# Other tile numbers for the side stages of a two-layer vision tower on one core

## The reference

```
h = tok(x, W)                                      # (16, 1024, 64)
h = h + attn0(layernorm(h), qkv, proj, bias_table) # scores + a bias of period 7
h = h + ffn0(layernorm(h), routed + shared)        # 128 hidden, 2 layers, ReLU
h = h + attn1(layernorm(h), qkv, proj)
h = h + ffn1(layernorm(h), top-2 of 8 experts)     # GELU, 128 hidden each
```

## Time and profile before

| | us |
|---|---|
| median of 3 runs | 4194.81 |
| lowest and highest | 4194.46, 4199.51 |
| the profiled execution, its own time | 4199.6 |
| its span, first to last instruction | 4197.8 |
| PE busy | 3900.1 (93%) |
| DVE busy | 2903.8 (69%) |
| ACT busy | 2638.1 (63%) |
| POOL busy | 857.9 (20%) |

### The profile page before, as it was taken

How to read it: one execution, slowest core, us unless ns; L and a number is a source line. 1 busy time by engine, 2 the same in 40 slices (tenths; PEclk the granted TensorE clock), 3 DMA queues, 4 the chain that set the end, 5 groups by cost and what they waited for, 6 DMA issues and landing times.

```text
span 4197.8 us, 62363 instructions
## 1 busy us (share of the span) xinstructions
PE 3900.1 (93%) x21508; PEld 1308.8 (31%) x21508; DVE 2903.8 (69%) x4955; ACT 2638.1 (63%) x4768; POOL 857.9 (20%) x1263
## 2 busy tenths in 40 slices
PE   6988999999999999999999999999999999999897
PEld 3223333332333323333333333323323333332222
DVE  4866767676776777757677776777767677677672
ACT  0656666666666666666666666666666666666564
POOL 4122212121211312212122121312212122121211
PEclk7999999999999999999999999999999999999998
DMA  5113201222112122111222112122111222111100
GB/s 103 37 31 56 39 21 31 51 40 42 34 34 41 31 42 49 36 25 31 42 48 42 33 35 41 31 42 49 33 27 31 42 49 42 30 31 28 23 10 6
DMA packets 119067, 156.36 MB, mean 37 GB/s; under 512 B 24847, under 2 KB 66575, under 8 KB 118717
## 3 DMA queue, kind: packets, MB, share of 16 engines
q1 hardware_dynamic: 118753, 152.38, 18.8%
HBM read 120.01 MB, written 29.36 MB: 36 GB/s over the span
## 4 chain that ended last, share of the span: by engine, by line
PE 68%; ACT 7%; POOL 7%; issue 6%; DVE 6%; DMA 2%; SPq 1%; POOLq 0%; ACTq 0%; DVEq 0%
PE acc L911 18%; PE side_st L897 18%; PE nat L885 15%; PE side_st L854 3%; DVE tile_max L1294 3%; PE side_st L750 2%; ACT hidden L1073 2%; POOL ln_s L1392 2%; ACT prob L1101 2%; PE side_st L840 2%; PE side_st L727 2%; PE side_st L807 1%; DMA q_rows<-max_rows 1%; ACT hidden L1019 1%; SPq L607 1%
## 5 line engine op out<-in xcount | busy, mean ns | idle before, releaser
L1294 DVE TENSOR_REDUCE tile_max<-nat 128x1 f32<-128x512 f32 x4096 | 2602.3, 683 | 1142.4 <-PE nat L885 1108.5
L1101 ACT ACTIVATE prob<-side_st 128x512 f32<-128x512 f32 x4096 | 2226.0, 600 | 1412.1 <-PE side_st L897 1373.7
L897 PE MATMUL side_st<-q_rows,k_rows 99*128 99x512 bf16 x4096 | 1578.4, 388 | 62.6 <-ACT prob L1101 32.3
L885 PE MATMUL nat<-k_rows,q_rows 96*128 96x512 bf16 x4096 | 1548.1, 389 | 35.8 <-DVE tile_max L1294 25.7
L911 PE MATMUL acc<-prob,v_padded 128*32 128x512 f32 x8192 | 1108.3, 613 | 6.0 <-ACT prob L1101 5.1
L897 PEld LDWEIGHTS side_st<-q_rows,k_rows 99*128 99x128 bf16 x4096 | 400.3, 99 | 1309.5 <-ACT prob L1101 903.9
L885 PEld LDWEIGHTS nat<-k_rows,q_rows 96*128 96x128 bf16 x4096 | 404.6, 99 | 529.8 <-DVE tile_max L1294 288.3
L1455 POOL TENSOR_SCALAR max_parts<-neg_max 128x16 bf16<-128x16 f32 x128 | 26.2, 205 | 1896.2 <-DVE neg_max L1301 1895.0
L911 PEld LDWEIGHTS acc<-prob,v_padded 128*32 128x32 f32 x8192 | 162.6, 108 | 376.7 <-ACT prob L1101 197.2
L840 PE MATMUL side_st<-ln_rows,w 64*128 64x512 f32 x512 | 140.1, 624 | 28.3 <-ACT hidden L1073 22.8
L1380 POOL TENSOR_SCALAR ln_s<-ln_s 128x8 f32<-128x8 f32 x64 | 12.9, 202 | 709.4 <-DVE ln_s L1202 705.7
(11 more groups left out here) (124 smaller groups left out, 2074.9 us busy)
## 6 DMA issues: line engine op xcount, KB each, us to landing
q_rows<-q_scratch SPq DMA_DIRECT2D x576, 64.0 KB
k_rows<-k_scratch SPq DMA_DIRECT2D x192, 192.0 KB
x_rows<-in_x SPq DMA_DIRECT2D x62, 512.0 KB, 6.5
q_scratch<-hidden SPq DMA_DIRECT2D x32, 384.0 KB
k_scratch<-hidden SPq DMA_DIRECT2D x96, 128.0 KB
group_weights<-in_routed SPq DMA_DIRECT2D x64, 129.0 KB, 2.1
q_rows<-max_rows SPq DMA_DIRECT2D x512, 3.0 KB
out_h<-out_rows SPq DMA_DIRECT2D x16, 256.0 KB, 2.1
```

What stands on the lines that cost most here:

```text
L885: eng.matmul(NAT[use % len(NAT)][:, :], QA[u][0:K_NAT, h, c:c + P], KA[u][0:K_NAT, h, kh * 512:kh * 512 + 512], start=True, stop=True)\
L897: eng.matmul(RING[TILE_BANK[n0 + n]][:, :], KA[u][0:K_ALL, h, t * P:t * P + P], QA[u][0:K_ALL, h, half * 512:half * 512 + 512], start=True ...
L1101: eng.activation(prob[:, n % TILES, :], RING[TILE_BANK[n0 + n]][:, :], ACT.Exp).then_inc(exp_done, 1)
L1294: eng.tensor_reduce(mx[:, q % 2, j // 8, j % 8 // 2, j % 2:j % 2 + 1], NAT[use % len(NAT)][:, :], AX.X, ALU.max).then_inc(nat_free, 1)
```

## The change

The numbers in `side_schedule` change, and nothing else. In `middle_of` the numbers count from tile 133: TR of LN "a" 161 to 162, H1 165 to 166, L0 170 to 171, L1 176 to 177, TR "1" 203 to 204, QK of the second layer 207 to 210, QV 212 to 213. In the tail of layer 1, TR goes from 31 to 33, GATE 35 to 36, RANK 41 to 43, MT 45 to 47, FW 48 to 50, FY0 to FY8 51 + 3k to 53 + 3k, OUT 82 to 85. For item r + 2, LN2 goes from 111 to 114, TR 119 to 123, QK 123 to 127, QV 127 to 131, VC 131 to 134, SCR 135 to 139, RL 144 to 147. WCA goes from 120 to 121.

```diff
         for dn, name, *more in ((0, "CT"), (5, "OTR"), (8, "PROJ", 0), (13, "LN1", "a"),
-                                (20, "LN2", "a"), (21, "BO"), (28, "TR", "a"), (32, "H1"), (37, "L0"),
-                                (43, "L1"), (49, "WO"), (56, "LN1", "1"), (62, "LN2", "1"),
-                                (70, "TR", "1"), (74, "QK", 1), (79, "QV", 1)):
+                                (20, "LN2", "a"), (21, "BO"), (29, "TR", "a"), (33, "H1"), (38, "L0"),
+                                (44, "L1"), (49, "WO"), (56, "LN1", "1"), (62, "LN2", "1"),
+                                (71, "TR", "1"), (77, "QK", 1), (80, "QV", 1)):
...
-        put(31, "TR", r - 1, "m")
-        put(35, "GATE", r - 1)
-        put(41, "RANK", r - 1)
-        put(45, "MT", r - 1)
-        put(48, "FW", r - 1)
+        put(33, "TR", r - 1, "m")
+        put(36, "GATE", r - 1)
+        put(43, "RANK", r - 1)
+        put(47, "MT", r - 1)
+        put(50, "FW", r - 1)
         for k in range(E + 1):
-            put(51 + 3 * k, f"FY{k}", r - 1)
-        put(82, "OUT", r - 1)
+            put(53 + 3 * k, f"FY{k}", r - 1)
+        put(85, "OUT", r - 1)
...
-        put(111, "LN2", r + 2, "0")
-        put(119, "TR", r + 2, "0")
-        put(123, "QK", r + 2, 0)
-        put(127, "QV", r + 2, 0)
-        put(131, "VC", r + 2, 0)
-        put(135, "SCR", r + 2, 0)
-        put(144, "RL", r + 2, 0, every=1)
+        put(114, "LN2", r + 2, "0")
+        put(123, "TR", r + 2, "0")
+        put(127, "QK", r + 2, 0)
+        put(131, "QV", r + 2, 0)
+        put(134, "VC", r + 2, 0)
+        put(139, "SCR", r + 2, 0)
+        put(147, "RL", r + 2, 0, every=1)
...
-        put(120, "WCA", r + 1)
+        put(121, "WCA", r + 1)
```

## The result

The changed kernel takes 4064.74 us (median of 4 runs, 4061.33 to 4069.15) beside 4195.88 us for the kernel before (median of 4 runs, 4194.46 to 4199.51): ratio 0.9687, interval 0.9670 to 0.9704, 131 us less. The direction and the mechanism came as forecast. The profiled execution took 4061.33 us, its span is 4059.6 us, and the mean granted clock 0.982.

The account below looks back on a forecast made before the run. PE, busy 93% of the span, was taken to set the pace. Large steps -5.3, small gains -2.2 and CT +0.6 made -6.9 us a pair, -97 in all: 4098 us, range 4070 to 4148.

Parts of the forecast that it names:

- The large steps: Second layer's QK and QV, tiles 207 to 215: stall, half clock and ACT wait go, QV waits; -5.3 us a pair.
- The half clock: Beside TN's stall at tile 215: the drop to 1.2 GHz goes with the stall, 2.5 us a pair.
- The forecast new waits: PE waits 1.1 us at QV (213) for ACT and 0.6 us at CT (133) for DVE.
- small terms: Waits at TN 119, TR 33 and 162, MT, OUT and tile 96 go: 2.9 us a pair, counted as 2.2.
- first layer's start: Tiles 111 to 147: TN's 0.58 us wait at 119 goes, CT at 133 gets a new wait of 0.6.
- the discount: Small gains counted at three quarters, 2.2 of 2.9 us, because a PE that waits less meets ACT and DVE less drained.
- the lower end: All small gains full, no wait at CT and 0.5 at QV: -8.8 us a pair, 4072; range from 4070.
- H1's new wait: At tile 169, for ACT's two copies: same size as the 0.73 us wait at 181 that goes, so they cancel.
- B: Rival: crowding at tiles 127 to 141 makes CT and `nat` wait and lowers the clock, +3.8 us a pair, 4151; chance 0.08.
- C: Rival: OUT's store holds up the maxima's transfers that tile 96's scores wait for; slower, 4225 us; chance 0.04.
- D: Rival: the split still stands behind POOL work at 209, only the small gains are left, about 4175 us; chance 0.04.
- A: Rival: the wait moves to QV (1.5 us) and TN (0.5), the half clock stays at tiles 210 to 216; 4146; chance 0.12.

Follow-up runs that it names:

- experiment 11: The changed kernel with six extra POOL products ahead of the split of the maxima at tile 209, once a pair: 4118.59 us, ratio 0.9826.
- experiment 1: The kernel before with only TR, QK and QV of the second layer moved, to 204, 210 and 213: 4114.79 us, ratio 0.9809.
- experiment 2: The changed kernel with TR, QK and QV of the second layer back at 203, 207 and 212: 4136.65 us, ratio 0.9855.
- experiment 3: The kernel before with only the tail of layer 1 moved (TR 33 to OUT 85): 4148.23 us, ratio 0.9883.
- experiment 5: The kernel before with only TR 162, H1 166, L0 171 and L1 177 moved: 4185.00 us, ratio 0.9970.
- Experiment 8: The changed kernel with H1 back at 165 and L0 at 170, L1 staying at 177: 4052.89 us, ratio 0.9656.
- experiment 10: The changed kernel with five extra POOL products ahead of the split of the maxima at tile 209, once a pair: 4100.81 us, ratio 0.9777.
- experiment 6: The changed kernel with QV of the second layer two tiles earlier, at 211: 4093.77 us, ratio 0.9753.

## Why the prediction was right, and where it was not

**The large steps held in their mechanism.** POOL's order at 209 was the cause of the stall at 215: with the order turned, TN waits for nothing, and six extra POOL operations ahead of the split bring a stall of 2.85 back (experiment 11). The half clock went with the stall in experiment 1 (3.4 us in one pair were left) and stood with it in experiment 2; the stall of 2.85 brought it back in a part of the pairs only. The forecast new waits came where they were named: 1.03 at QV (forecast 1.1, from ACT's 1.44 of copies in the earlier trace rows), 0.77 at CT (forecast 0.6, bounds 0 to 1.2). TR, MT and OUT show no wait at 33, 47, 85 and 162. What the sum lacked is size, in its small terms above all:

| place in a pair | forecast, us | measured, us |
|---|---|---|
| late stages, tiles 192 to 223 | -5.3 | -6.1 |
| tail and tile 96, tiles 16 to 95 | 2.07 x 3/4 = -1.6 | -3.1 |
| first layer's start, tiles 112 to 143 | -0.58 x 3/4 + 0.6 = +0.2 | 0.0 |
| middle, tiles 160 to 191 | -0.29 x 3/4 = -0.2 | -0.6 |
| a pair | -6.9 | -9.8 |

Measured is the median over pairs 2 to 12 of the spacing of scores, segment by segment. Over the whole profiled execution pairs 1 to 13 give 126 us (forecast 90), pair 0 gives 7.0 (5), the last pair and phase 3.1 (2), and the start, the first phase and the end 2.4 (0): together 138.

Of the 2.9 us a pair that the sum lacked, the discount took some 0.7, the brackets read as full prices 0.9, and the half clock priced too low 0.5. The 0.8 that is left are gaps to which the prediction gave no term. Each of these follows.

**The discount failed: "of which I count three quarters".** Its reason was that a PE that waits less meets ACT and DVE less drained. A little of the kind did come. In the tail two waits stand that were not there, for DVE at tile 40 and for ACT at tile 84. Timeline of PE, kernel after:

```profile
1481.90 0.39 PE L885 MATMUL nat<-k_rows,q_rows 96*128 96x512 bf16 x1 [0.16 <-DVE tile_max L1294]
...
1540.47 0.39 PE L897 MATMUL side_st<-q_rows,k_rows 99*128 99x512 bf16 x1 [0.17 <-ACT prob L1101]
```

But the tail, priced at 2.07 undiscounted, still gave 3.3 a pair in experiment 3. That DVE at 71% and ACT at 65% of the span have the slack for it is the likely reason, not one that a run isolated. The discount alone doesn't account for the miss: without it the sum gives 4088, still 23 us above what was measured. Nor does it account for the range: the lower end, -8.8 a pair, took all small gains in full, no wait at CT and 0.5 at QV, and -9.8 was measured with the waits at CT and QV there. The prices themselves were too low.

**The brackets were read as full prices, and they are too short by 0.16.** The timeline shows a matmul of scores or `nat` as 0.38 long, but the next one starts 0.22 behind it when nothing is late. Timeline of PE, kernel after:

```profile
1637.35 0.38 PE L885 MATMUL nat<-k_rows,q_rows 96*128 96x512 bf16 x1
1637.57 0.38 PE L897 MATMUL side_st<-q_rows,k_rows 99*128 99x512 bf16 x1
```

The idle time behind such a matmul is counted from its modelled end, so a bracket behind it hides 0.38 - 0.22 = 0.16 of the true loss. Timeline of PE, kernel before, tile 214 to 215:

```profile
1713.41 0.38 PE L885 MATMUL nat<-k_rows,q_rows 96*128 96x512 bf16 x1
...
1717.29 0.29 PE L869 MATMUL side_st<-ident_b,max_parts 128*128 128x128 bf16 x1 [3.50 <-POOL max_parts L1461]
```

Here 1717.29 - 1713.41 = 3.88, less 0.22 is 3.66, not 3.50. On one wait that is little; the tail has four or five of them. (OUT's is behind a `pv` and hides 0.06.) It was to be seen in the trace before.

**A wait was overlooked.** At tile 39, between GATE (35) and RANK (41), `nat` waited for DVE in the kernel before:

```profile
1530.54 0.39 PE L885 MATMUL nat<-k_rows,q_rows 96*128 96x512 bf16 x1 [0.38 <-DVE tile_max L1294]
```

With 0.16 it is 0.54, and in the kernel after it has shrunk to the 0.16 at tile 40 shown above, 0.32 with the hidden part. With the `nat` beside it this place gives 0.37. The prediction saw that RANK gets "a tile more behind GATE" and gave it no term. That the one tile is the cause is argued from the two timelines, and was not tried alone. At tiles 87 and 88 two gaps ahead of `nat`, too short to show a bracket, are gone too, 0.36; the wait at tile 84 costs 0.34. From start to start the tail then gives 0.73 (TR) + 0.37 + 0.66 (MT) + 0.51 (OUT) + 0.36 + 0.78 (tile 96) - 0.34 = 3.1, beside 3.1 to 3.3 measured.

**The half clock was priced from a short pair.** The prediction read 8.95 - 6.21 = 2.7 in pair 5 and took 2.5. Pair 9 of the kernel before has 9.19:

```profile
2727.14 0.29 PE L869 MATMUL side_st<-ident_b,max_parts 128*128 128x128 bf16 x1 [3.50 <-POOL max_parts L1461]
...
2736.33 0.38 PE L897 MATMUL side_st<-q_rows,k_rows 99*128 99x512 bf16 x1
```

Most pairs are like this, and against 6.21 it makes 2.98. Experiment 11 gives the same from the other side: 248.75 - 245.75 = 3.0 for 6.8 us at half clock. Rounding down went the wrong way, and no run shows the reason given for it, that the super compared with has no copy of the values near it.

**The middle was right by neither count.** The prediction let H1's new wait cancel the one at tile 181. The waits shown went from 0.29 + 0.44 + 0.73 = 1.46 to 0.36 + 1.23 = 1.59, so by them the middle should have lost a little; it gained 0.6, in the change and alone (experiment 5). From start to start the same waits come to 0.45 + 0.59 + 0.90 = 1.94 before and 0.43 + 1.40 = 1.83 after, a gain of 0.1. Another 0.2 comes from L0 and L1: two of their groups of four matmuls (L807) stood right behind a `pv` and took 0.97 each; none stands there now, and each takes 0.86. About 0.1 more comes from H1, which stood between two `nat` and stands behind a `pv` now. The rest is gaps of 0.2 and less, which stay open. Experiment 8 shows that the move of H1 itself was a loss inside that gain: back at 165 it saves 0.7 a pair.

**The rivals.** B (the crowd at 127 to 141) is refuted: CT waits 0.77, `nat` has no new waits, the clock stays. C (the maxima's transfers late at tile 96) is refuted: the only long wait of that kind is still the 7.8 of pair 0. D is refuted by the order on POOL. A is refuted for this change, with one drop in thirteen pairs, and borne out beside it: two tiles less at QV and the clock falls in nine pairs of thirteen. The Trainium skill, "TensorE: Matmul & The Clock Gate", Part 1, holds that the throttled state is the default and activity releases it. The prediction drew from it that one stall doesn't decide. For 3.50 us the traces speak against that reading: that stall brought a drop 65 times of 65. For shorter ones the length alone doesn't settle it (1.6 us: eight of thirteen, 2.85 us: four, and FW's 1.49 never). What does decide between two pairs that do the same work these runs don't show, and neither do they show whether it is the length of 3.50 or the work around it that brought a drop each time.

## What to carry to other kernels

Where an engine runs its program in order, look for a long piece of side work that starts just before a short piece which another engine waits for: here one wrong order on POOL, which is busy for a fifth of the span, cost PE 6.6 us a pair, nearly half of it through the clock. Price a wait by the spacing of starts with and without it, not by the idle time shown, and take it from several repeats. Here most of what small waits cost was gained when they went, with a quarter of the other engines' time free. When a stage is moved off one wait, move it only as far as the order needs (209, not 210): the tile was worth 12 us in the profiled executions and 16 in the medians.

## What was not expected of the hardware

- **The same stall, the same work, another clock.** With waits of 1.90 at QV the clock fell in nine of thirteen pairs, with 1.61 at TN in eight (in two of them ahead of TN), with 2.85 in four, with 3.50 in all thirteen of each of five kernels, and with 0.33 in none. With the same 1.03 at QV it fell once in the kernel after, once in experiment 1 and three times in experiment 8. FW's wait for the GELU, 1.49 us at tile 50 (48 before), stands in each of these thirteen pairs of every kernel, and no drop came beside it. A wait that is shorter than another is not for that reason safer, and the place counts, too.
- **Between pairs 1 and 13 a drop comes in two lengths, with two prices.** 3.4 us at 1.2 GHz cost 1.4 to 2.3 us in experiments 5, 10 and 11 and about 1 in experiment 6 (once 2); 6.8 us cost 3.0 in the kernel before and in experiment 11 and 2.6 to 3.1 in experiment 6, but about 2 in experiment 10, where QV's wait and TN's lay inside it.
